# Zero-padded high parts, column groups for two small products, and a new step order in a fused conv-attention-routing kernel

## The reference, cut to what matters

```
x = conv_layer(x)           # 32 batches of 128 channels x 1024 positions
#   bcdt = w_bcdt @ channel_norm(x); 3x3 grouped conv -> BC, dt (32 rows each)
#   AB = softmax(dt + A) * BC
#   h = x @ AB^T (128x32);  y = w_out @ (h @ BC) + x
t = tokens(x)               # 32768 tokens of 128 values
t = t + attention(ln(t))    # per batch of 1024 positions, one head
#   q, k = lrelu(u Wq + bq), lrelu(u Wk + bk)  (64 wide);  v = lrelu(u Wv + bv)  (128 wide)
#   out = softmax(mask(q k^T / 8)) v + u;  layer norm with gamma, beta
t = t + experts(ln(t))      # top-1 of 8 experts, 128 -> 512 -> 128
#   logits = u gate_w + gate_b; slot = count of earlier tokens of that expert
#   capacity 5120 tokens an expert; result times the gate's probability
```

## Time and profile before

| | |
|---|---|
| runs of the kernel before | 2498.07, 2505.41, 2508.59 us |
| median | 2505.41 us |
| the profiled execution, its own time | 2497.93 us |
| its span, first to last instruction | 2496.2 us |
| mean granted TensorE clock | 0.934 of 2.4 GHz |
| PE busy | 88% |
| DVE busy | 75% |
| ACT busy | 47% |
| POOL busy | 40% |

### The profile page before, as it was taken

The page is one execution under the profiler, slowest core; times in us unless marked ns, Lnnn a source line. Parts: engine busy times, 40 slices in busy tenths (PEclk is TensorE's granted clock), DMA queues, the critical chain, the costliest instruction groups (busy, mean ns, idle before and its releaser), DMA issues. The chain is left out here.

```text
span 2496.2 us, 42793 instructions
## 1 busy us (share of the span) xinstructions
PE 2197.8 (88%) x14047; PEld 1785.5 (72%) x14047; DVE 1878.5 (75%) x6062; ACT 1167.5 (47%) x2184; POOL 1009.8 (40%) x1262
## 2 busy tenths in 40 slices
PE   2699999999999999999999999998749999999945
PEld 1477777777777777777777777777648888888834
DVE  3468878887878888778888788887548888887822
ACT  0144544544434444445444445444237776766712
POOL 2012443334443334533334433343436565555510
PEclk9699999999999999999999999999869999999965
DMA  6711211112211112211112111111046666666568
GB/s 228 275 35 43 67 46 44 52 47 54 64 44 52 44 47 59 58 43 52 44 52 68 45 46 49 44 48 49 18 123 184 192 187 190 180 189 175 139 223 315
DMA packets 163512, 243.97 MB, mean 98 GB/s; under 512 B 31039, under 2 KB 110478, under 8 KB 163296
## 3 DMA queue, kind: packets, MB, share of 16 engines
q1 hardware_dynamic: 141408, 192.68, 27.0%
q0 software_dynamic: 17280, 31.84, 3.9%
q10 hardware_dynamic: 4608, 16.78, 1.7%
HBM read 115.95 MB, written 95.56 MB: 85 GB/s over the span
## 5 line engine op out<-in xcount | busy, mean ns | idle before, releaser
L995 PE MATMUL pvp<-va,pT 128*128 128x129 f32 x4096 | 536.2, 287 | 1.4 <-ACT pT L556 1.4
L995 PEld LDWEIGHTS pvp<-va,pT 128*128 128x128 f32 x4096 | 514.9, 203 | 11.3 <-ACT pT L556 3.0
L1124 POOL DMA_INDIRECT token_rows<-res x284 | 312.9, 1102 | 234.8 <-DVE res L1235 162.3
L654 DVE TENSOR_REDUCE mxs<-mxp 128x1 f32<-128x512 f32 x512 | 333.9, 683 | 21.7 <-PE mxp L873 17.5
L1281 PEld LDWEIGHTS e_yp<-w2s,hid 128*128 128x128 f32 x2272 | 294.6, 192 | 71.0 <-ACT hid L1170 48.7
L1281 PE MATMUL e_yp<-w2s,hid 128*128 128x128 f32 x2272 | 306.2, 278 | 27.8 <-ACT hid L1170 26.8
L470 POOL DMA_INDIRECT expert_slots<-rows,slot_i x256 | 273.8, 1069 | 97.5 <-issue 91.7
L427 POOL TENSOR_TENSOR rstd<-var,neghalf 128x4 f32<-128x4 f32 x128 | 131.0, 1023 | 396.5 <-DVE negm L645 396.1
L556 ACT ACTIVATE pT<-stp 128x512 f32<-128x512 f32 x512 | 277.6, 595 | 17.2 <-issue 9.4
L967 PE MATMUL stp<-qhl,klh 128*128 128x512 f32 x512 | 237.0, 463 | 27.4 <-ACT pT L556 14.2
L1170 ACT ACTIVATE hid<-e_hp,b1c 128x512 f32<-128x512 f32 x284 | 193.1, 680 | 144.6 <-PE e_hp L1273 132.6
(11 more groups left out here) (222 smaller groups left out, 4278.3 us busy)
## 6 DMA issues: line engine op xcount, KB each, us to landing
w1p<-w_parts SPq DMA_DIRECT2D x71, 512.0 KB
expert_slots<-fill SPq DMA_DIRECT2D x32, 660.0 KB, 12.7
e_rows<-expert_slots SPq DMA_DIRECT2D x71, 264.0 KB
w2s<-in_w SPq DMA_DIRECT2D x71, 256.0 KB
xs<-in_x SPq DMA_DIRECT2D x32, 512.0 KB, 3.7
token_rows<-rows SPq DMA_DIRECT2D x32, 512.0 KB
f_rows<-token_rows SPq DMA_DIRECT2D x32, 512.0 KB, 5.8
out<-f_cols ACTq DMA_DIRECT2D x32, 512.0 KB, 5.4
```

What stands on the lines that cost most here:

```text
L654: v.reduce_max(mxs[:, qt, n % 2:n % 2 + 1], mxp[n % 2][:], AX).then_inc(s["mx_read"], 1)
L995: last = mm(pvp[qt % 2][:, 0:VA], pT[c][:, kt, n * P:(n + 1) * P], va[k][:, kt, :], start=(kt == 0), stop=(kt == NT - 1))
L1124: g.indirect_dma_start(out=tokens, out_offset=bass.IndirectOffsetOnAxis(ap=res[n % 2][:, q, TOKEN:TOKEN + 1].bitcast(I32), axis=0), in_=re ...
```

## The change

Four things change, all in `token_program`.

`qhi` and `khi` get 128 rows instead of 66. Rows 65 to 126 of `qhi` are zero and those of `khi` one, so they add nothing; the negated maximum moves from row 65 to row 127. `mx` takes 127 rows and `st` 128.

`h` writes its eight products to four groups of 32 PSUM rows instead of adding all to rows 0 to 31. Two products add in each group, and the sum of the four groups is made by `hh`, whose loaded `hT` now has 128 rows and whose identity is stacked four times.

`gate` swaps its operands. The gate's weights (padded to 32 columns) are loaded, and the tokens stream through in four products of 256 columns, each to its own 32 rows of `mxp[0]`. ACT copies the result (`lgT`, 128x256), PE transposes it in two pieces into `mxp[1]` in a new step `gate_turn`, and DVE's chain and ACT's `eg` follow that.

The order of `steps` is new, and the first and the last passes are written out as lists of their own (`head`, `tail`), in which the steps of the batches interleave in another way than in the middle. The same 29 passes stand between them.

```
-KA = U + 2
+TOP = P - 1
-        hT = sb("hT", [S, C])
+        hT = sb("hT", [P, C])
-        qhi = [sb(f"qhi{k}", [KA, N], F32R) for k in range(2)]
-        khi = [sb(f"khi{k}", [KA, N], F32R) for k in range(2)]
+        qhi = [sb(f"qhi{k}", [P, N], F32R) for k in range(2)]
+        khi = [sb(f"khi{k}", [P, N], F32R) for k in range(2)]
...
-        steps = ["x_turn", ("mx", 1, 0), ("mx", 1, 1), ("st", 0, 0), ("st", 0, 1), ("xs", 0), ("u1n", 3),
+        steps = [("u1n", 3), ("mx", 1, 0), "x_turn", ("st", 0, 0), ("st", 0, 1), ("mx", 1, 1), ("st", 0, 2),
...
             for d in range(2):
-                chain(g.affine_select(out=ident2[:, d * S:(d + 1) * S], in_=ident2[:, d * S:(d + 1) * S], pattern=[[-1, S]],
-                                      compare_op=ALU.not_equal, fill=1.0, base=0, channel_multiplier=1))
+                for j in range(Q4):
+                    own = ident2[:, d * S:(d + 1) * S]
+                    chain(g.affine_select(out=own, in_=own, pattern=[[-1, S]], compare_op=ALU.not_equal, fill=1.0,
+                                          base=-j * S, channel_multiplier=1))
...
+            chain(g.memset(gwc[:], 0.0))
...
-                chain(g.memset(qhi[k][U:KA, :].bitcast(F32), 1.0))
-                chain(g.memset(khi[k][U:KA, :].bitcast(F32), 1.0))
+                chain(g.memset(qhi[k][U:P, :].bitcast(F32), 0.0))
+                chain(g.memset(qhi[k][U:U + 1, :].bitcast(F32), 1.0))
+                chain(g.memset(khi[k][U:P, :].bitcast(F32), 1.0))
...
                 if st == "gate":
+                    act.wait_ge(s["gate_done"], b + 1)
+                    if not first:
+                        act.wait_ge(s["gate_turned"], b)
+                    a.copy(lgT[:], mxp[0][:, 0:2 * P]).then_inc(s["lgT_ready"], 1)
+                if st == "gate_turn":
                     act.wait_ge(s["gate_chain"], b * GL + 3)
...
-                        last = mm(work[0:S, 1, 0:C], abT[:, jj, e * S:(e + 1) * S], xT[:, t, :], start=(t == 0), stop=(t == NT - 1))
+                        last = mm(work[jj * S:(jj + 1) * S, 1, 0:C], abT[:, jj, e * S:(e + 1) * S], xT[:, t, :],
+                                  start=(e == 0), stop=(e == 1), tile_position=(0, jj * S))
...
-                    if not early(b, 1):
-                        pe.wait_ge(s["gate_chain"], b * GL - 2)
-                    pe.wait_ge(s["o_ready"], B * 8 if isinstance(b, int) and b == B - 1 else b * 8 + 15)
-                    for t in range(NT):
-                        last = mm(pvp[0][:, GATE + t * E:GATE + (t + 1) * E], u2T[:, t * P:(t + 1) * P], gwc[:], start=True, stop=True)
+                    pe.wait_ge(s["nt_ready"], min(b * 2 + 5, 2 * B))
+                    for j in range(Q4):
+                        last = mm(mxp[0][j * S:(j + 1) * S, 0:2 * P], gwc[:], u2T[:, j * 2 * P:(j + 1) * 2 * P],
+                                  start=True, stop=True, tile_position=(0, j * S))
                     last.then_inc(s["gate_done"], 1)
+                if st == "gate_turn":
+                    pe.wait_ge(s["lgT_ready"], b + 1)
+                    for h in range(2):
+                        last = nc.tensor.transpose(mxp[1][:, h * P:(h + 1) * P], lgT[:, h * P:(h + 1) * P], ident[:])
+                    last.then_inc(s["gate_turned"], 1)
```

More of the change, by code:

```diff
@@ L206, in bc_mid @@
             return ap2.unsqueeze(1).to_broadcast([ap2.shape[0], n, ap2.shape[1]])
-        steps = ["x_turn", ("mx", 1, 0), ("mx", 1, 1), ("st", 0, 0), ("st", 0, 1), ("xs", 0), ("u1n", 3),
[10 rows of a table removed]
-        ROUTE = ("ln2s", "ln2n", "ln2g", "ln3s", "u2_turn", "gate")
+        steps = [("u1n", 3), ("mx", 1, 0), "x_turn", ("st", 0, 0), ("st", 0, 1), ("mx", 1, 1), ("st", 0, 2),
+                 ("st", 0, 3), ("xs", 0), "u1_turn", ("mx", 1, 2), ("st", 0, 4), "kflag", ("st", 0, 5), ("mx", 1, 3),
+                 ("xs", 1), "qk", ("st", 0, 6), ("mx", 1, 4), ("st", 0, 7), "pos", "v", ("mx", 1, 5), ("pv", 0, 0),
+                 "bcdt", ("mx", 1, 6), ("mx", 1, 7), ("negmax", 1), ("pv", 0, 1), "bT_turn", ("mrow", 1),
[7 rows of a table added]
+        ROUTE = ("ln2s", "ln2n", "ln2g", "ln3s", "u2_turn", "gate", "gate_turn")
         LATE = ("pos", "scatter")
@@ L226, in token_program, with batch, one_pass @@
         ATT = ("t1b", "st", "pv", ("mx", 1), ("negmax", 1), ("mrow", 1))
-        def batch(i, c):
-            return i * 2 + c, i + c // 2, c % 2
-        def one_pass(one, i, c, attend=True, last=False):
+        def batch(b):
+            return b, b // 2, b % 2
+        head = [(0, ("xs", 0)), (0, "x_turn"), (0, ("xs", 1)), (0, "bcdt"), (0, "bT_turn"), (0, "dt"), (0, "conv"),
[3 rows of a table added]
+                (0, "mask"), (1, "bT_turn"), (0, "qk_lrelu"), (1, "conv"), (0, "qk_high"), (1, "dt"), (0, "qk_low"),
[3 rows of a table added]
+                (0, ("negmax", 0)), (2, "x_turn"), (1, ("ts", 0)), (1, ("u1n", 2)), (0, ("mrow", 0)),
[5 rows of a table added]
+                (2, "bcdt"), (0, ("negmax", 1)), (0, ("pv", 0, 1)), (0, ("mrow", 1)), (2, "bT_turn"),
[8 rows of a table added]
+        tail = [(2, ("st", 0, 0)), (2, ("st", 0, 1)), (1, ("u1n", 3)), (2, ("mx", 1, 0)), (2, ("mx", 1, 1)),
[24 rows of a table added]
+                (1, ("ln3s", 1)), (2, "scatter"), (1, "gate_turn"), (1, "scatter"), (1, "pos")]
+        def one_pass(one, c):
             for st in steps:
@@ L236, in one_pass @@
                 if any(n in ATT for n in names):
-                    if attend:
-                        one(st, *batch(i, c))
+                    one(st, *batch(c))
                 elif any(n in ROUTE for n in names):
-                    if attend and c != 0:
-                        one(st, *batch(i, c - 1))
+                    one(st, *batch(c - 1))
                 elif any(n in LATE for n in names):
-                    if attend and not early(i * 2 + c, 2):
-                        one(st, *batch(i, c - 2))
+                    if c >= 2:
+                        one(st, *batch(c - 2))
                 elif any(n in PROJ for n in names):
-                    if c != -2 and not (last and c == B - 1):
-                        one(st, *batch(i, c + 1))
-                elif not last:
-                    one(st, *batch(i, c + 2))
+                    one(st, *batch(c + 1))
+                else:
+                    one(st, *batch(c + 2))
         def passes(eng, one):
-            one_pass(one, 0, -2, attend=False)
-            one_pass(one, 0, -1, attend=False)
-            one_pass(one, 0, 0)
-            one_pass(one, 0, 1)
-            one_pass(one, 0, 2)
-            for i in range(1, (B - 4) // 2):
-                one_pass(one, i, 1)
-                one_pass(one, i, 2)
-            one_pass(one, 0, B - 3)
-            one_pass(one, 0, B - 2, last=True)
-            one_pass(one, 0, B - 1, last=True)
-            for st in steps:
-                if st in LATE:
-                    one(st, *batch(0, B - 2))
-                elif (st[0] if isinstance(st, tuple) else st) in ROUTE:
-                    one(st, *batch(0, B - 1))
-            for st in LATE:
-                one(st, *batch(0, B - 1))
+            for b, st in head:
+                one(st, *batch(b))
+            for c in range(1, B - 2):
+                one_pass(one, c)
+            for back, st in tail:
+                one(st, *batch(B - back))
         block = ctx.enter_context(nc.Block())
@@ L699, in one @@
                     dve.wait_ge(s["hT_done"], b + 1)
-                    v.tensor_copy(hT[:], work[0:S, 1, 0:C]).then_inc(s["hT_ready"], 1)
+                    v.tensor_copy(hT[:], work[:, 1, 0:C]).then_inc(s["hT_ready"], 1)
                 if st == "hh":
@@ L785, in one @@
                     negmax(b, j)
-                if st == "gate":
+                if st == "gate_turn":
                     gc = s["gate_chain"]
```

28 lines of the change are left out of this document (18 added, 10 removed), and 60 rows, old and new, of tables (head, steps, tail).

## The result

The changed kernel takes 2428.07 us (median; runs 2416.41, 2427.87, 2428.28, 2431.05), the kernel before 2505.41 (median of four): a ratio of 0.9687, 95% interval 0.9649 to 0.9725. It is 77 us faster; the forecast was 71, at 2434. The profiled execution is the one of 2431.05, with a span of 2429.3.

What follows compares the result with a forecast made beforehand. PE was taken as the bound (88% of the span, DVE 75%). Terms 38 + 20 + 3 + 7 + 3 = 71 us off the profiled 2497.9 gave 2427, stated as a median of 2434; range 2392 to 2490.

Steps and rivals of the forecast that it cites:

- quiet passes: `conv` to next `conv`, 51.84 us before; forecast 1.3 us shorter each, 38 us over 29 passes.
- clock: Falls of PE's granted clock, at two places in the passes, cost 29 us; 20 of them forecast to go.
- head: Start of the token program: constants plus 4.0, three `h` minus 3.5, interleaving minus 3.5; sum minus 3 us.
- behind the last `conv`: End of the token program: tail minus 7 us with scatters moved behind, two more passes ahead of it minus 3.
- PE's work: Products in a pass: `h` minus 0.78, `gate` minus 0.70, two transposes plus 0.30; sum minus 1.2 us.
- rival D: All four column groups overlap, `h` and `gate` at a quarter of 1.94 each: 2395 us, quiet pass 49.2; chance 0.14.
- A: The main forecast, all terms as summed: median 2434 us, quiet pass 50.5; chance 0.48.
- The gate: Gate on PE: products minus 0.70, transposes plus 0.30, wait for ACT's copy plus 0.75 us a pass.
- The third `st`: PE's wait at the third `st`, as the first exponential comes later: 1.5 us in place of 0.33.
- Waits that go: PE's waits in a pass: ahead of `h` minus 0.68, at `g` minus 0.2, at the eighth `mx` minus 0.82 us.
- Rival E: The falls of the clock stay, 20 us less gained: 2454 us; chance 0.14.
- Rival C: Clock falls at the new waiting place behind `gate`, at most 3.4 us a pass: 2524 us, slower; chance 0.08.

Runs made afterwards that it cites:

- experiment 2: Changed kernel with `h` put back to one group of 32 PSUM rows (`hT` of 32 rows): 2349.55 us, ratio 0.973 to the kernel before.
- experiment 3: Changed kernel with the gate's operands put back, no `lgT` and no transposes: 2316.81 us, ratio 0.9593 to the kernel before.
- experiment 12: Changed kernel with only the last two normalisations of u1 moved behind the first two `st`: 2389.76 us, ratio 0.9593 to the kernel before.
- experiment 5: The kernel before, unchanged, traced again on another chip, which showed no standstill: 2413.94 us.
- experiment 9: Changed kernel with one more DVE instruction (1.22 us) ahead of the copy to `hT`: 2402.93 us, ratio 0.9662 to the kernel before.
- experiment 11: Changed kernel with `gate_turn` behind the next pass's first two `st`, and two normalisations behind it: 2440.14 us, ratio 0.9798 to the kernel before.
- experiment 1: Changed kernel run again without edit, on a second chip: 2307.84 us, ratio 0.9558 to the kernel before.
- experiment 8: Changed kernel with first and last passes made by the old rule instead of own lists: 2326.68 us, ratio 0.9644 to the kernel before.
- experiment 4: Changed kernel without the rows of zeros (`qhi` and `khi` of 66 rows): 2325.54 us, ratio 0.9626 to the kernel before.
- experiment 7: Kernel before with the new order of steps alone, without `gate_turn`, ends by the old rule: 2422.64 us, ratio 1.0052 to the kernel before.
- experiment 10: Kernel before with `h` in four groups and the rows of zeros: 2440.56 us, ratio 0.9802 to the kernel before.
- experiment 6: Kernel before with only `h` changed to four groups: 2407.82 us, ratio 0.9989 to the kernel before.

## Why the prediction was right

The forecast's sum was 71 and the profiled executions differ by 67. Term by term, forecast and measured: quiet passes 38 and 66, clock 20 and minus 5, head 3 and 4, behind the last `conv` 10 and 10, experts' part 0 and minus 8. The direction and the ends were right for the reasons given. That the sum came out is luck: two large terms were wrong by 28 and 25, with opposite signs.

**PE's work: under-sized.** The mechanism was right, the factor was not. I took `y`'s 1.16 for `h` and for the gate. But `y` has two groups, and its records start two at a time; those of `h` in four groups start four at a time: 0.58 to the next start where one group takes 1.87 (experiment 2), a factor of 3.2. That was rival D's premise, and its number for a quiet pass, 49.2, is nearer to 49.57 than A's 50.5. The argument against D, that two records in a row go to one group, did not hold. The Trainium skill (TensorE: Matmul & The Clock Gate, Part 3) has matmuls on different column groups run at the same time, with 2.38 for three of them; the trace agrees and four give 3.2 here. The price of a change of tiling, which the prediction left open, takes nothing from the gain: from the last record of `h` to the next start are 0.20 us where it is 0.11 behind a `pv`, and `h` in one group had the same.

**The gate: wrong in sign.** Minus 0.70, plus 0.30, plus 0.75 made the pass 0.35 longer; measured from gate to `mx` it is 0.32 shorter (1.72 to 1.40), of which the quiet pass keeps 0.1 (experiment 3). Products 1.1 less, wait 0.57, transposes 0.19: each term had its sign, and each was off.

**The third `st`.** 1.19 for the 1.5 that I gave, for the reason that I gave (experiment 12: 0.44 without the normalisations). The working there does not give 1.5: a path of 3.5 less 2.4 of work is 1.1, close to what was measured. At the `st` behind `conv` I added 0.7; that wait was there before and only went from 0.46 to 0.55.

**Waits that go.** Those ahead of `h`, at `g` and at the eighth `mx` went, as said, though the first not for the reason given: it was the standstill's and not `abT`'s own (experiment 5). All together a pass is 2.27 shorter and not 1.3, over 29 passes 66 us and not 38. One new wait was not seen, 1.13 ahead of `hh`. Its origin stood in the earlier trace rows, the 1.96 "remote" at `exT`: I passed over the row's bracket. It was a standstill that ends with the scatters' landing on this chip, and the new order moved another part of the chain under it, from `exT` (0.68 at PE) to `hT` (1.13). Where there is none, the change is worth 2.83 a pass (51.11 to 48.28) and 106 us in all (0.9558), outside what A allowed and near D.

**The clock: wrong.** I took 20 of 29 us away; beyond quiet passes the 26 take 34.7, 5 more than before. Of the two places, the one behind `bcdt` went (9 falls before, none after, by the granted clock), and the one at `y` filled up (10 before, 17 after), 15 of them right behind the 1.13 wait and two ahead of it. The time at 1.2 GHz in the 26 passes only went from 78.5 to 68.2 us. Rival E had the clock right on this chip, and not the sum. Windows around one of the 15 falls, changed kernel:

```profile
557.90:561.30 3.40, 2.22 (x12) 1.09 (x10) 2.13 (x7) 0.00 (x0) 3.15 (x3) 1.00 0.08 25
561.30:564.70 3.40, 3.40 (x24) 2.98 (x24) 2.91 (x7) 0.00 (x0) 2.13 (x7) 0.61 0.00 0
```

PE was busy 2.22 of 3.40 at 2.4 GHz (wait, `hh`, `mx`, `g`), and then a granted clock of 0.61 follows, mostly 1.2 GHz. On the chip without the standstill the same kernel has no such stretch in 26 passes and loses 3.5 us. That the standstill causes the rest is argued from this and not shown: with a wait of 1.0 to 1.1 ahead of `hh`, experiments 9, 12 and 11 lost 13, 22 and 31, and without the standstill, with the rows of zeros and the new order, experiments 1, 2, 3 and 8 had no fall in the 26 passes. But the chips differ in more than the standstill, as the experts' part shows. Nor did I see that the rows of zeros matter. I gave them no price and left their effect on the clock open; experiment 4 has it at 17.7 us. Rival C's mechanism is real too, but not at its place: a fall behind a wait of 1.86 at the third `st` in 8 of 26 passes (experiment 7), none behind 1.19.

**The head.** DVE's first work starts at 22.66, forecast 22.3, so the constants cost 4.4. Up to the sixth `conv` it is minus 10.6, of which three full passes are 6.8; the head proper gives 3.8, forecast 3.

**The tail.** Forecast 35.5 from the last `pv` to the end of the last scatter; measured from the end of the last two `pv`, which run together from 1720.04 to 1723.78, to 1759.42, 35.6 (42.8 before, also from the end: 1791.80 is where the gate behind the last `pv` starts). Timeline of POOL, changed kernel:

```profile
1757.17 0.97 POOL L510 DMA_INDIRECT expert_slots<-rows,slot_i  x1 [0.30 <-issue]
1758.45 0.97 POOL L510 DMA_INDIRECT expert_slots<-rows,slot_i  x1 [0.30 <-issue]
```

Sixteen in a row, 1.28 apart, where I counted 1.27; the whole stretch behind the last `conv` gave 10.4 for the 10 forecast.

**The parts do not add.** In the kernel before, `h` alone is worth 0.1% and the order alone costs 0.5%. Together with gate, rows and ends they give 4.4% on the same kind of chip. `h` alone brings a fall of the clock into nearly every pass, and in the changed kernel, with rows and new order, on the same kind of chip, there is no fall with `h` in four groups or in one (experiments 1 and 2). Whether it needs both is open: with the rows but in the old order it gave 2.0%, on a chip with the standstill (experiment 10). The order needs the gate's chain behind the normalisations (1.86 at the third `st` in experiment 7, 1.08 with the same old gate and the chain one step later in experiment 3), and lists of its own at the ends.

## What to carry to other kernels

When a product is taken off a PE-bound pass, read the granted clock again before counting the gain: here a shorter `h` was answered with a fall of the clock that took nearly all of the gain back (experiment 6). An idle time whose releaser is not one of the program's engines belongs in the sum like any other: find what ends it (here a DMA's landing), and ask what the new order puts there. Small products that each fill a quarter of the columns are worth dealing out over all four groups (1.87 to 0.58 us here), and a change of several parts should be priced together, since each part alone may show nothing.
